# A fused attention and ternary feed-forward layer: loop skewed by one or two steps, token rows loaded before weights, output projection moved into the second feed-forward matmul

## The chip, the cores and the metric

One Trainium2 chip, all 8 NeuronCores; each core computes one of the 8 sequences of the batch (2048 tokens of 1024 features) and needs nothing from the others. The metric is the device time in microseconds of the slowest core. Shown is the median of three runs.

## The reference

```python
xn  = layernorm(x)                                  # x: (8, 2048, 1024)
q, k = xn @ Wq.T, xn @ Wk.T                         # 16 heads of 16 features
v   = xn @ Wv.T                                     # 16 heads of 64
f(z) = [1, z / 2, outer(z, z) / (4 * sqrt(2))]      # 273 features of a head
A   = tril(f(q) @ f(k).T)                           # (2048, 2048) for each head
y   = rms_norm(A @ v) * g_weight                    # over the 64 of each head
attn = y @ Wo.T
tern(W) = clip(round(W / s), -1, 1), s = max(mean(abs(W)), 1e-8)
ffn = gelu(xn @ tern(W1).T + b1) @ tern(W2).T + b2  # 1024 -> 4096 -> 1024
out = x + attn + ffn
```

## The kernel before, in words

The order of the work on each engine is written out by hand, one function an engine (`sync_stream`, `gp_stream`, `vec_stream`, `sca_stream`, `ten_stream`); semaphores connect them. DMAs are issued from SP (tokens, transposes, q blocks, stores) and from POOL (weights, which are cast from float32 to bfloat16 on the way when they go to `wqk`, `wv` and `wo`). Every queue is worked off in order: a wait at its head holds all that is behind it.

**Start.** SP loads token tiles of 128 rows into `xr` (three buffers); VectorE takes mean and variance (L447, L448, L450), ScalarE the root (L676), VectorE the reciprocal and the normalised rows `xn_tm` (L458), and SP transposes them by DMA into `xnT` (L264). The first projections (L772) need four tiles. POOL has issued all attention weights and the first two 1 MB staging loads by then (L348 to L373).

**Attention loop.** 32 iterations `i`: 16 chunks of 128 tokens for each half of the heads (8 heads). The sum over the past is held as a state in PSUM (`pST`), so a chunk needs its own 128 x 128 scores and the state before it. Iteration `i` on TensorE: scores of chunk i (L828); v (L784) and spread k (L793) of chunk i+1; y from the state (`y_before`, L841 to L853), spread q of i+1 (L804), y within the chunk (`y_within`, L862), spread q, update of the state (L872, L877), the small spread q (L815); in one iteration of four the q and k of the next block of four chunks (L772). ScalarE squares the scores (L722: a second-order polynomial by one square with bias), empties v, kx and the spread q (L681, L685, L691, L697), squares y (L735) and copies the state (L739). VectorE masks the squared scores (L586), makes the k features (`features_k`), raw q (L499), the sum of squares (L600), the scaled y (L511) and the second part of the state (L605). SP copies q into a block-diagonal `qblk` (eight copies a block, L275), which the scores read. All projections share two banks of `pW` in turn ("units": a table fixes their order; a unit waits until the one two before it is emptied).

In the loop ScalarE also sums the absolute values of `W1` (L709, `A1_SLOTS`, for the ternary threshold), and from iteration 18 on TensorE does the output projection of one finished chunk an iteration (`proj_out`, L891: 16 matmuls), VectorE adds x to it (`empty_wo`, L526) and SP writes the sum to DRAM (`res_scr`). Each y is transposed by DMA into `yT` (L282). The last two chunks' projections stand between the first steps of the next stage.

**Up** (`up`, L954): 32 steps `j` of 2 x 16 matmuls of `w1t`, the ternary weights that VectorE makes in two passes (L544, L547); ScalarE applies gelu (L751) into `hT` and sums absolute values of `W2`. Four PSUM pairs rotate.

**Down** (`down`, L977): for each half of the 1024 outputs, 16 groups `n` of 32 matmuls. The first eight groups run together, one step of `j` after another, each in a PSUM bank of its own; the other eight one after another. VectorE adds `b2` to what SP has read back from `res_scr` (L661), adds the PSUM bank (L667), and SP stores (L330). All 16 ternary `w2t` tiles but the last have their own place.

## Time and profile before

| | before |
|---|---|
| median of the runs | 809.74 us (805.32 to 813.83, 3 runs) |
| the profiled execution | 806.29 us, its slowest core's span 804.8 us |
| spans of the 8 cores | 799.1 to 804.8 us |
| mean granted clock of TensorE | 0.976 to 0.983 of full speed |
| TensorE, VectorE, ScalarE, GpSimd busy | 689.8 (86%), 376.4 (47%), 285.1 (35%), 40.6 us (5%) |
| DMA | 124.78 MB, mean 155 GB/s |

The span runs from the first to the last instruction of the slowest core. A busy share is the time in which at least one instruction of the engine is under way; matmuls are pipelined, so that several are under way together. The profile's line numbers (L828) are those of the kernel before.

### The profile page before, as it was taken

What the parts mean: (1) busy time and instruction counts of PE and PEld (TensorE: products, weight loads), DVE (VectorE), ACT (ScalarE), POOL (GpSimd) and SP (SyncE); (2) the same over time, 40 slices, a digit from 0 to 9 for tenths busy, and PEclk for the clock granted to TensorE, in tenths of its full rate; (3) what the DMA queues carried; (4) which work ended last, traced back from release to release, by engine and by line L of the source; (5) the groups of instructions that cost most, each with busy time, mean ns of one, the idle gap of its engine ahead of it and who ended that gap; (6) DMA issues with size and microseconds to landing.
All of it is one profiled execution on the core that took longest, in us unless ns stands there. A gap on an engine that the chain in (4) does not pass through costs nothing.

```text
span 804.8 us, 11638 instructions; the slowest of 8 cores (799.1 to 804.8 us)
## 1 busy us (share of the span) xinstructions
PE 689.8 (86%) x3996; PEld 330.3 (41%) x3996; DVE 376.4 (47%) x652; ACT 285.1 (35%) x432; POOL 40.6 (5%) x77
## 2 busy tenths in 40 slices
PE   0037776775899999879999999999999999999998
PEld 0013443442444444434444444444444444444443
DVE  4238886765666666752131314453366433300342
ACT  0006565673866765423556554333300000000000
POOL 2000000000000000000111111000010000000000
PEclk9999998998999999999999999999999999999999
DMA  8956674447679895663566664534154565100562
GB/s 150 235 128 134 129 137 104 145 88 155 179 227 240 218 246 150 170 205 110 198 233 210 224 216 189 177 136 158 53 187 135 175 157 157 53 1 1 140 165 88
DMA packets 62904, 124.78 MB, mean 155 GB/s; under 512 B 38528, under 2 KB 39552, under 8 KB 54272
## 3 DMA queue, kind: packets, MB, share of 16 engines
q0 software_dynamic: 10080, 72.62, 29.6%
q1 hardware_dynamic: 52768, 51.41, 25.8%
q8 instruction: 35, 0.57, 0.3%
q14 instruction: 21, 0.17, 0.1%
HBM read 103.30 MB, written 16.78 MB: 149 GB/s over the span
## 4 chain that ended last, share of the span: by engine, by line
PE 74%; DMA 9%; DVE 6%; issue 5%; ACT 3%; SPq 2%; DVEq 0%; ACTq 0%; POOL 0%; POOLq 0%
PE pW L891 7%; PE pST L954 7%; PE pSS L954 7%; PE pST L977 7%; PE pY L977 7%; PE pW L977 7%; PE pSS L977 7%; PE pY L954 6%; PE pW L954 6%; PE pW L784 4%; DMA xr<-x 4%; PE pW L772 2%; DMA wo_sb<-wo 2%; ACT qf L691 2%; SPq L275 2%
## 5 line engine op out<-in xcount | busy, mean ns | idle before, releaser
L772 PE MATMUL pW<-xnT,wqk_sb 128*128 128x512 bf16 x128 | 30.9, 398 | 57.6 <-DMA xnT<-xn_tm 51.6
L544 DVE TENSOR_SCALAR w1t<-stg,consts 128x2048 bf16<-128x2048 f32 x16 | 20.5, 1283 | 104.2 <-DMA stg<-w1r 84.8
L784 PE MATMUL pW<-wv_sb,xnT 128*128 128x512 bf16 x256 | 66.1, 405 | 0.4
L977 PE MATMUL pST<-w2t,hT 128*128 128x512 bf16 x256 | 66.0, 379 | 0.1
L977 PE MATMUL pW<-w2t,hT 128*128 128x512 bf16 x256 | 66.0, 379 | 0.0
L977 PE MATMUL pSS<-w2t,hT 128*128 128x512 bf16 x256 | 66.0, 379 | 0.0
L977 PE MATMUL pY<-w2t,hT 128*128 128x512 bf16 x256 | 66.0, 379 | 0.0
L709 ACT ACTIVATE stg<-stg 128x2048 f32<-128x2048 f32 x32 | 60.8, 1899 | 13.0 <-DMA stg<-w2r 13.0
L891 PE MATMUL pW<-wo_sb,yT 128*128 128x512 bf16 x256 | 60.7, 392 | 5.0 <-ACT qf L691 3.9
L954 PE MATMUL pST<-xnT,w1t 128*128 128x512 bf16 x272 | 61.5, 379 | 0.0
L954 PE MATMUL pSS<-xnT,w1t 128*128 128x512 bf16 x272 | 61.5, 379 | 0.0
L722 ACT ACTIVATE Am<-pSS,consts 128x1024 bf16<-128x1024 f32 x32 | 35.4, 1106 | 60.4 <-PE pSS L828 60.3
L954 PE MATMUL pY<-xnT,w1t 128*128 128x512 bf16 x240 | 54.2, 379 | 0.4 <-DVE consts L531 0.4
L954 PE MATMUL pW<-xnT,w1t 128*128 128x512 bf16 x240 | 54.2, 379 | 0.0
L661 DVE TENSOR_TENSOR res<-res,b2bc 128x512 f32<-128x512 f32 x32 | 22.1, 690 | 45.7 <-DMA res<-res_scr 45.5
L772 PEld LDWEIGHTS pW<-xnT,wqk_sb 128*128 128x128 bf16 x128 | 12.5, 101 | 73.4 <-issue 61.3
L784 PEld LDWEIGHTS pW<-wv_sb,xnT 128*128 128x128 bf16 x256 | 26.0, 104 | 38.1 <-issue 14.2
L544 DVE TENSOR_SCALAR w2t<-stg,consts 128x2048 bf16<-128x2048 f32 x16 | 20.5, 1283 | 44.2 <-PE pST L954 26.6
L691 ACT ACTIVATE qf<-pW 128x512 bf16<-128x512 f32 x64 | 35.0, 592 | 17.4 <-PE pW L804 17.1
L526 DVE TENSOR_TENSOR rst<-pW,xre 128x512 f32<-128x512 f32 x32 | 22.1, 691 | 38.5 <-PE pW L891 38.5
L891 PEld LDWEIGHTS pW<-wo_sb,yT 128*128 128x128 bf16 x256 | 24.9, 100 | 36.3 <-issue 10.3
L954 PEld LDWEIGHTS pSS<-xnT,w1t 128*128 128x128 bf16 x272 | 26.6, 98 | 32.1
(121 smaller groups left out, 921.5 us busy)
## 6 DMA issues: line engine op xcount, KB each, us to landing
stg<-w1r POOLq DMA_DIRECT2D x32, 1024.0 KB, 6.7
stg<-w2r POOLq DMA_DIRECT2D x32, 1024.0 KB, 6.2
xr<-x SPq DMA_DIRECT2D x16, 512.0 KB, 5.3
xre<-x SPq DMA_DIRECT2D x16, 512.0 KB, 6.1
res_scr<-rst SPq DMA_DIRECT2D x16, 512.0 KB, 4.3
res<-res_scr SPq DMA_DIRECT2D x32, 256.0 KB, 4.2
out<-osb SPq DMA_DIRECT2D x32, 256.0 KB, 2.7
wv_sb<-wv POOLq DMA_DIRECT2D x2, 1024.0 KB, 22.1
```

Of the source, the lines that this page charges most:

```text
L275: e.dma_start(out=qblk[16 * h:16 * h + 16, B % 2, h, :], in_=qT[16 * h:16 * h + 16, B % 2, :]).then_inc(dQB, 16)
L526: e.tensor_tensor(rst[:, c % 2, sl], work_bank(UID[key]), xre[:, c % 2, sl], ALU.add).then_inc(dW, 1)
L544: e.tensor_single_scalar(dst, src, cc(col + 1), ALU.is_lt).then_inc(sTA, 1)
L661: e.tensor_tensor(res[:, n % 2, :], res[:, n % 2, :], b2bc[:, dh * 512:dh * 512 + 512], ALU.add).then_inc(dRB, 1)
L691: e.activation(qf0[:, i % 2, 4 * half:4 * half + 4, :].rearrange("p h f -> p (h f)"), work_bank(UID[key]), AF.Square).then_inc(aW, 1)
L709: e.activation(buf, buf, AF.Abs, accum_out=cc(col)).then_inc(done, 1)
L722: e.activation(Am[:, b, :, :].rearrange("p h f -> p (h f)"), pSS[:], AF.Square, bias=cc(C_BI), scale=SC).then_inc(aSQ, 1)
L772: mm = e.matmul(work_bank(u), wqk[:, hf, kd, o:o + 128], xnT[:, 4 * b:4 * b + 4, kd, :], start=(kd == 0), stop=(kd == KD - 1))
L784: mm = e.matmul(work_bank(u), xnT[:, c, kd, :], wv[:, hf, kd, :], start=(kd == 0), stop=(kd == KD - 1))
L891: mm = e.matmul(work_bank(u), yT[:, c, k, :], wo[:, k, 512 * dh:512 * dh + 512], start=(k == 0), stop=(k == KD - 1))
L954: mm = e.matmul(ps[:, 512 * half:512 * half + 512], w1t[:, j % 6, kd, :], xnT[:, 4 * tb:4 * tb + 4, kd, :], start=(kd == 0), stop=(kd == K ...
L977: return e.matmul(out_bank(n), hT[:, j, 128 * t:128 * t + 128], w2t[8 * dh + j // 4][:, j % 4, :], start=(j == 0), stop=(j == NJ - 1))
```

## The change

- **Loop.** `scores(i + 1)` is issued in iteration i behind `outputs(i)` (which is `y_before` and `y_within` in one), v and kx of chunk i+2, `update(i)` first. v has three buffers. q is spread once for a block of four chunks: eight units `qf` of one 512-column matmul and a `qg` (q_units), in place of `qfa`, `qfb`, `qf1` in each iteration; raw q is copied by two DMAs from SP. `kx` of a chunk after which no state is needed is left out.
- **Layer norm.** The normalisation moves from VectorE to ScalarE (`normalise`, function Identity with scale and bias); `xr` has four buffers.
- **Start.** Token loads are the first DMAs on SP. On POOL come the iotas, the first half of q/k and v weights, four memsets that VectorE did before, then q blocks: half of block 0, blocks 1 and 2, with the second halves of the weights between, and only then the staging loads, with the other q blocks among them (`BEFORE_LOAD`).
- **Absolute sums.** The 16 of `W1` are at iterations 9 to 24, alternately on ScalarE and on VectorE (`tensor_reduce`).
- **Projection.** No `proj_out`, `empty_wo`, `res_scr`. y is stored to DRAM (`y_scr`, bfloat16); in the down stage it is read back by transposing DMAs, four tiles deep, once for each half of the outputs; after the 32 matmuls of a group come 8 of `yT` x `wo` in the same PSUM group (`attn`). `wo` is loaded and scaled half by half. x is read from the input in place of `res_scr`.
- **w2t.** Nine tiles have a place of their own; tiles 9 to 15 are made when the first half of the outputs is complete.

```diff
+def q_units(i, place):
+    if i == 0:
+        return {"first": [("qf", 4), ("qf", 5)], "mid": [("qf", 6)],
+                "last": [("qf", 7), ("qg", 0)]}[place]
+    B = i // 4 + 1
+    if B > 7:
+        return []
+    table = {1: {"first": [], "mid": [("qg", B)],
+                 "last": [("qf", 8 * B), ("qf", 8 * B + 1)]},
+             2: {"first": [("qf", 8 * B + 2)], "mid": [("qf", 8 * B + 3)],
+                 "last": [("qf", 8 * B + 4)]},
+             3: {"first": [("qf", 8 * B + 5)], "mid": [("qf", 8 * B + 6)],
+                 "last": [("qf", 8 * B + 7)]}}
+    return table.get(i % 4, {}).get(place, [])
+BEFORE_LOAD = {("a1", 0): ("b1", 0), ("a1", 2): ("q", 3), ("a1", 6): ("q", 4),
+               ("a1", 10): ("q", 5), ("a1", 14): ("q", 6), ("t1", 2): ("q", 7),
+               ("t2", 9): ("wo", 0), ("t2", 11): ("wo", 1)}
...
 def sync_stream(e):
-        e.dma_start(out=cc(C_G), in_=g_d).then_inc(dC, 16)
-        e.dma_start(out=consts[:, C_B1:C_B1 + 32], in_=b1_d).then_inc(dC, 16)
...
+        def y_in(n):
+            t = n % 16
+            if n >= 4:
+                e.wait_ge(pO, n - 3)
+            dYT.inc(e.dma_start(
+                out=yT[:, n % 4, :, :],
+                in_=y_scr[t * 128:(t + 1) * 128, :].rearrange(
+                    "p (b i) -> p b i", b=KD, i=128),
+                transpose=True), n)
...
         for n in range(32):
             final_out(n)
+            if n + 4 < 32:
+                y_in(n + 4)
             if n + 2 < 32:
-                res_in(n + 2)
+                x_again(n + 2)
...
 def gp_stream(e):
+        e.dma_start(out=wqk[:, 0, :, :], in_=wqk_d[0]).then_inc(dQK[0], 16)
         e.dma_start(out=wv[:, 0, :, :], in_=wv_d[0]).then_inc(dV[0], 16)
+        e.memset(qblk[:].rearrange("p a h t -> p (a h t)").bitcast(F32),
+                 0.0).then_inc(sMS, 1)
...
+        q_block(e, 0, range(4, 8), dQB)
+        q_block(e, 1, range(8), dQB)
         e.dma_start(out=wqk[:, 1, :, :], in_=wqk_d[1]).then_inc(dQK[1], 16)
+        q_block(e, 2, range(8), dQB)
         e.dma_start(out=wv[:, 1, :, :], in_=wv_d[1]).then_inc(dV[1], 16)
...
+            elif what == "wo":
+                if which == 0:
+                    e.wait_ge(pH, 2 * NJ)
+                else:
+                    e.wait_ge(pO, 16)
+                e.dma_start(out=wo[:], in_=wo_d[which]).then_inc(dWO[which], 16)
...
 def vec_stream(e):
         for i in range(NI):
+            if i + 1 < NI and has_state(i + 1):
+                features_k(i + 1)
+            if has_state(i):
+                state_out(i)
+            if new_block(i) is not None:
+                empty_qk("q", new_block(i))
+                empty_qk("k", new_block(i))
             for t in ln_tiles(i):
+                ln_stats(t)
+            if i >= 1:
+                rms_and_scale(i - 1)
+            for t in ln_tiles(i):
+                ln_scale(t)
+            sum_squares(i)
+            if i + 1 < NI:
+                mask(i + 1)
...
+            if n == 16:
+                for u in range(9, 16):
+                    ternary2(u)
+                scale_wo(1)
...
 def sca_stream(e):
         for i in range(NI):
+            if has_state(i):
+                e.wait_ge(pU, updates(i))
+                e.mul(st0[:, (i + 1) % 2, :], pST[:, 0:512], 1.0 / 32).then_inc(aS0, 1)
+            empty_q(q_units(i, "first"))
             e.wait_ge(pYD, i + 1)
             e.activation(ysq[:, b, :], pY[:, 512 * b:512 * b + 512],
                          AF.Square).then_inc(aYS, 1)
...
+            if i + 2 < NI:
+                empty_v(i + 2)
             if i + 1 < NI:
+                square(i + 1)
+            empty_q(q_units(i, "mid"))
+            if kx_chunk(i) is not None:
+                empty_kx(i + 2)
+            empty_q(q_units(i, "last"))
+            for t in ln_tiles(i):
+                normalise(t)
+            rms_sqrt(i)
...
 def ten_stream(e):
         for i in range(NI):
+            if has_state(i):
                 update(i)
+            if new_block(i) is not None:
+                proj_qk("q", new_block(i))
+                proj_qk("k", new_block(i))
+            spread_q(q_units(i, "first"))
+            outputs(i)
+            if i + 2 < NI:
+                proj_v(i + 2)
+            if i + 1 < NI:
+                scores(i + 1)
+            spread_q(q_units(i, "mid"))
+            if kx_chunk(i) is not None:
+                spread_k(i + 2)
+            spread_q(q_units(i, "last"))
...
+        def attn(n):
+            dh = n // 16
+            dYT.wait_done(e, n)
+            e.wait_ge(sWOG, KD * (dh + 1))
+            for k in range(KD):
+                mm = e.matmul(out_bank(n), yT[:, n % 4, k, :], wo[:, k, :],
+                              start=False, stop=(k == KD - 1))
+            mm.then_inc(pO, 1)
...
+            for n in range(n0, n0 + 8):
+                attn(n)
             for n in range(n0 + 8, n0 + 16):
                 down_free(n)
                 for j in range(NJ):
-                    mm = down(n, j)
-                mm.then_inc(pO, 1)
+                    down(n, j)
+                attn(n)
```

## Rows read from the trace of the kernel before

**Rows 1.** Windows by stage: length, busy us of each engine, granted clock, DMA share, GB/s.
```profile
0.00:26.00 26.00, 0.00 (x0) 0.00 (x0) 13.23 (x39) 1.87 (x3) 4.43 (x14) 1.00 0.91 161
26.00:51.60 25.60, 0.00 (x0) 0.01 (x1) 4.74 (x10) 0.59 (x2) 0.00 (x0) 1.00 0.95 229
51.60:128.70 77.10, 55.36 (x457) 28.41 (x457) 60.77 (x148) 43.10 (x88) 0.53 (x1) 0.97 0.62 130
128.70:220.40 91.70, 68.14 (x578) 36.59 (x579) 57.40 (x143) 63.30 (x114) 4.22 (x8) 0.90 0.52 128
220.40:351.40 131.00, 116.72 (x880) 61.53 (x879) 83.66 (x177) 73.52 (x128) 5.28 (x10) 0.97 0.78 206
351.40:580.20 228.80, 228.39 (x1060) 103.72 (x1059) 76.92 (x51) 101.66 (x96) 21.22 (x36) 1.00 0.51 177
580.20:805.00 224.80, 221.18 (x1025) 100.00 (x1022) 79.63 (x84) 1.11 (x1) 4.92 (x8) 1.00 0.39 113
```

**Rows 2.** Timeline, 0 to 60 us: start, duration in us, instruction, idle time before.
```profile
41.27 0.69 DVE L447 BATCH_NORM_STATS2 consts<-xr 128x6 f32<-128x512 f32 x1 [12.58 <-DMA xr<-x]
...
46.00 1.23 SPq L264 DMA_TRANSPOSE xnT<-xn_tm  x1
...
51.62 5.65 PE L772 MATMUL pW<-xnT,wqk_sb 128*128 128x512 bf16 x16 [51.62 <-DMA xnT<-xn_tm]
```

**Rows 3.** Timeline of TensorE in the attention loop.
```profile
62.53 0.97 PE L828 MATMUL pSS<-qblk,kT 128*128 128x512 bf16 x2 [1.11 <-DMA qblk<-qT]
...
128.74 1.01 PE L828 MATMUL pSS<-qblk,kT 128*128 128x512 bf16 x2 [5.15 <-DMA qblk<-qT]
...
220.40 3.62 PE L891 MATMUL pW<-wo_sb,yT 128*128 128x512 bf16 x16
```

**Rows 4.** Groups by form, ScalarE: count, busy us, mean ns, idle before.
```profile
L709 ACT ACTIVATE stg<-stg 128x2048 f32<-128x2048 f32 x32 | 60.8, 1899 | 13.0 <-DMA stg<-w2r 13.0
L722 ACT ACTIVATE Am<-pSS,consts 128x1024 bf16<-128x1024 f32 x32 | 35.4, 1106 | 60.4 <-PE pSS L828 60.3
L691 ACT ACTIVATE qf<-pW 128x512 bf16<-128x512 f32 x64 | 35.0, 592 | 17.4 <-PE pW L804 17.1 <-issue 0.2
...
L681 ACT CAST v<-pW 128x512 bf16<-128x512 f32 x32 | 18.5, 579 | 29.1 <-PE pW L784 29.0
...
L703 ACT ACTIVATE consts<-consts 128x8 f32<-128x8 f32 x32 | 9.3, 291 | 3.5 <-DVE consts L600 3.5
...
L676 ACT ACT_TABLE_LOAD x1 | 1.3, 1283 | 15.2 <-DVE consts L450 15.2
```

**Rows 5.** Groups by form, VectorE.
```profile
L547 DVE SCALAR_TENSOR_TENSOR w2t<-stg,consts,w2t 128x2048 bf16<-128x2048 f32 x16 | 37.6, 2352 | 2.0 <-DVE w2t L544 0.5
...
L544 DVE TENSOR_SCALAR w2t<-stg,consts 128x2048 bf16<-128x2048 f32 x16 | 20.5, 1283 | 44.2 <-PE pST L954 26.6 <-DMA stg<-w2r 17.6
...
L458 DVE TENSOR_SCALAR xn_tm<-xr,consts 128x1024 bf16<-128x1024 f32 x16 | 13.0, 812 | 1.7
```

**Rows 6.** Chain of waits, down stage: start, us, what; 64 matmuls in one piece.
```profile
773.82 13.81 PE pSS L977 x64
```

**Rows 7.** Timeline of VectorE after the first eight groups of down.
```profile
641.53 0.69 DVE L661 TENSOR_TENSOR res<-res,b2bc 128x512 f32<-128x512 f32 x1 [5.10 <-DMA res<-res_scr]
```

**Rows 8.** DMA issues: KB each, median us to landing.
```profile
wv_sb<-wv POOLq DMA_DIRECT2D x2, 1024.0 KB, 22.1
wo_sb<-wo POOLq DMA_DIRECT2D x1, 2048.0 KB, 19.2
wqk_sb<-wqk POOLq DMA_DIRECT2D x2, 512.0 KB, 15.0
...
xnT<-xn_tm SPq DMA_TRANSPOSE x16, 3.7
```

**Rows 9.** Groups by form, POOL's DMA issues.
```profile
L373 POOL DMA_DIRECT2D stg<-w2r x32 | 18.3, 571 | 198.3 <-DVE w2t L547 91.0 <-DVE w1t L547 74.2 <-ACT stg L709 33.1
```

**Rows 10.** Tile xn_tm, the DMA that reads it (the transpose into xnT).
```profile
DMA to landing us min/median/max: 3.1/3.7/16.7
```

More of the change, by code:

```diff
@@ L247, in ln_tiles, with q_block, x_in @@
         if i == 0:
[L248 to L250 removed]
+            return (6, 7)
+        if i <= 8:
+            return (i + 7,)
         return ()
+    def q_block(e, B, heads, done):
+        e.wait_ge(dW, D_DONE[UID[("q", B)]])
+        for h in heads:
+            e.dma_start(out=qblk[16 * h:16 * h + 16, B % 2, h, :],
+                        in_=qT[16 * h:16 * h + 16, B % 2, :]).then_inc(done, 16)
     def sync_stream(e):
[L255 to L258 removed]
+        def x_in(t):
+            dX.inc(e.dma_start(out=xr[:, t % 4, :],
+                               in_=x_d[t * 128:(t + 1) * 128, :]), t)
         def xn_out(t):
@@ L652, in vec_stream @@
         ternary1(15)
-        for u in range(3, 15):
+        for u in range(3, 9):
             ternary2(u)
+        e.wait_ge(dC, 32)
+        scale_wo(0)
         e.wait_ge(dB2, 16)
@@ L822, in scores @@
+        def scores(n):
+            B, c4 = n // 4, n % 4
             if c4 == 0:
-                e.wait_ge(dQB, 128 * (B + 1))
+                e.wait_ge(dQS, 64)
+                e.wait_ge(dQB, 64 + 128 * B)
                 e.wait_ge(dW, D_DONE[UID[("k", B)]])
-            if i >= 1:
-                e.wait_ge(aSQ, i)
-            for n in range(2):
-                mm = e.matmul(pSS[:, 512 * n:512 * n + 512],
+            if n >= 1:
+                e.wait_ge(aSQ, n)
+            for m in range(2):
+                mm = e.matmul(pSS[:, 512 * m:512 * m + 512],
@@ L873, in update @@
                          kf0[:, b, h, :, :].rearrange("p o i -> p (o i)"),
-                         v[:, b, E * h:E * h + E], start=(first and h == 0),
+                         v[:, i % 3, E * h:E * h + E], start=(first and h == 0),
                          stop=True, skip_group_check=True)
@@ L994, in ten_stream @@
                 for j in range(NJ):
[L995 to L996 removed]
+                    down(n, j)
+                attn(n)
     with ctx:
```

818 lines of the change are left out of this document (376 added, 442 removed).

## The prediction, made before the result was known

> **What bounds the kernel now.** I first cut the span into stages [rows 1]. TensorE starts at 51.6 us; the attention loop runs to 351.4, the first feed-forward matmul (up) to 580.2, the second (down) to the end. Both feed-forward stages are solid TensorE at full clock, 228.39 of 228.8 us busy and 221.18 of 224.8: they can only change by the number of matmuls. The rest is 351 us, and there TensorE is idle for the first 51.6 and then, in the three stretches of the loop, for 21.7, 23.6 and 14.3 us. "Busy" flatters it: a pipelined matmul shows as 0.4 us but streams 512 columns in 13.81/64 = 0.216 us [rows 6], so the loop has more slack than that, hidden in bubbles of small matmuls.
>
> Then the timeline. In the start [rows 2] VectorE gets the fourth token tile only at 41.27, after a wait of 12.58 us for its load; DMA is over 90% busy all that time [rows 1], carrying weights that nobody needs yet. The loop [rows 3]: scores of iteration 0 at 62.53, of iteration 8 at 128.74 (8.3 us an iteration, the last with a wait of 5.15 us for the q blocks), and the first output projection, of iteration 18, at 220.40: 157.9 us for 19 iterations. From 220.4 to 351.4 there are 14 pairs of output projections of 16 matmuls (16 x 0.216 = 3.45 us each, 48.3 in all), so the rest of these iterations takes 131.0 - 48.3 = 82.7 us, or 6.4 for each of 13.
>
> **Start.** Before TensorE's start DMA moves 26 x 161 + 25.6 x 229 GB/s = 10 MB [rows 1]. Of these, the second q/k and v weights, the bias row and two 1 MB staging loads now wait in POOL's queue behind copies of q blocks, which wait for q itself. Left are four tiles of 128 x 1024 in float32, 2.1 MB, and 1.5 MB of weights as landed [rows 8]: at 161 to 195 GB/s (the mean of the two) 19 to 23 us. So the fourth tile lands near 22; statistics 2 x 0.69 [rows 2], small operations about 1, the scaling 1.1, the transpose 3.7 (median) to 5.6 (issued at 46.00, used at 51.62) [rows 2, 8]: TensorE starts at 30, bounds 26 (tokens landing before the weights) and 38 (a transpose that lands in 12 us, within the 16.7 of [rows 10]). **-21.6 us.** The memsets that move to POOL are covered as long as they end before the q blocks are filled, some 30 us later.
>
> **Loop.** The skew puts scores one iteration ahead and k features and v two, so that TensorE no longer waits for square, mask and features in one chain; the pace is then set by the fullest engine.
> - ScalarE, each iteration [rows 4]: square of scores 1.11, v 0.58, kx, ysq and state of the same 512 columns and so 0.6 each, q features 2 x 0.59, the root of the rms 0.3; sum 4.97. New: the small q features, two instructions a block of four iterations, of at most 0.59 us: 0.3 an iteration, sum 5.25. In the first nine iterations a root 0.3 and the normalisation that DVE loses: no row has it on ScalarE; between 0.59 (512 wide) and 1.90 (2048 wide), nearest the 1024 wide square, 1.1. Sum 6.65. In iterations 9 to 24 every second one carries an absolute sum, 1.90 and its read-out 0.2: 1.05 on average, sum 6.3. Back-to-back instructions overlap a little, some 0.06 each, so 6.1, 5.8 and 4.8.
> - VectorE had 60.77 busy us in the first stretch [rows 1], some 7 an iteration; it loses 0.81 (scaling) and 0.43 (raw q, now two small copies on SP): about 6. Later it takes eight absolute sums; no row has such a reduction of 2048; between 1.28 (a 2048 wide operation) and 2.35 [rows 5], 2.2 because its reductions run one element a cycle like the latter: 1.1 an iteration, on 4.1 (6 less the statistics): 5.2.
> - TensorE: v 1.73, the rest some 11 streams of 512 columns, 2.4, and q and k 3.45 in one iteration of four: 5.0 on average but 8 in that one, which nothing can overtake because the two work banks are shared.
> The iterations with q and k are TensorE's (8.0), the others ScalarE's or VectorE's (6.0 to 7.0). I take 6.8, 6.5 and 5.8 for the three phases (9, 16 and 7 iterations, the last with two ternary stalls): 61 + 104 + 41 = 206, and 14 ahead of it (before 10.9; one more v and kx, clock at half): 220 us, bounds 190 (TensorE's own 5.0 with half an us of bubbles each) and 245. Before it is 299.8 - 48.3 = 251.5 without projections. **-31.5 us.** Most comes from the first half; in the second the projections were also cover, under which ScalarE did its absolute sums, so that removing 48.3 us there doesn't bring 48.3 by itself; that is in the 206.
>
> **Projection.** Moved, not removed: 256 matmuls, 55.2 us, out of loop (48.3) and up (6.9), into down. **0.** VectorE's 32 additions of 0.69 us and the residual's trip to DRAM go, all hidden.
>
> **Down, its waits.** After the first eight groups, eight projections of 1.73 us follow at once, but only four transposed tiles fit. Load 4 waits for projection 0; loads 6 and 7 stand in SP's queue behind the store of outputs 2 and 3, which wait for an addition that waits for x. That round trip is in the trace: after two quick evictions the third waits 5.10 us for its load [rows 7]. Counted from the start of projection 0: it ends at 1.7, is evicted at 2.6, SP issues store, transpose and x load until 4.5; x lands some 5 later, the addition and eviction of output 2 take 1.4, so load 6 is issued at about 11.5 us and load 7 at 13.5. With a landing of L the last projection ends at 15.2 + L, against 13.8 unhindered, so the loss is L + 1.4. L is 3.7 at the median for the same shape out of SBUF, 3.1 at least and 16.7 at most [rows 8, 10]; from DRAM it has no row. With 4.2, near the median, 5.6 us, and some at half clock: 6 each, twice. **+12 us** (9 to 36). The second half's loads of `w2` now come after the first half is done; VectorE makes one in 1.28 + 2.35 = 3.6 us, TensorE uses one in 6.9. The tightest is the third new one, whose load starts at 4.5 us and must be ternary at 20.7, behind 1 MB of landed `wo`; cover 2 us. If `wo` took its 19.2 us of before [rows 8], it costs 9.
>
> **Sum.** 804.8 - 21.6 - 31.5 + 12 = 763.7 of span; its execution took 1.5 more than the span, and the median of the runs is 0.4% above it: **767 us**.
>
> **ScalarE's tables.** The row shows one load of 1.28 us for roots, squares, copies and absolute values together [rows 4]. The normalisation adds a function, Identity. The Trainium skill, ScalarE: Activation LUTs, section "Table sets: the hidden batching unit", says that such cheap functions are in every set, so no load is added. If it were otherwise, 16 tiles with two loads each are 41 us, most of them seen: 805.
>
> **Rivals.**
> 1. TensorE's pace: the loop reaches 5.5 an iteration, 190 in all: 767 - 30 = 737. For it: slack averages out over four iterations. Against: two work banks, both emptied by ScalarE in strict order. 0.13.
> 2. ScalarE or VectorE in the way: the bubbles between engines stay, 7.2 an iteration: 245, so 792. For it: ScalarE is at 6.65 of work in the first phase, 1 us more than now. 0.14.
> 3. The start isn't earlier: x loads stay slow because a queue gives them the same share beside the weights; TensorE at 45: 782. Against: the weights are a third as many. 0.07.
> 4. Slower: q blocks through POOL. Sixty of the 64 small copies leave SP for POOL's queue. In the trace POOL issues a DMA in 0.57 us [rows 9], with VectorE busy 64% of the last loop stretch [rows 1], so eight take 4.6 us; some 13 us lie between q and the scores that need it. It decides from 13/8 = 1.6 us an issue. Were each issue held by one ternary operation of 2.35 us [rows 5], it took 2.9, eight 23.4, and TensorE waited 10 us in each of seven blocks: 767 + 73 = 840; over 817 from 2.5 us an issue on. 0.03. The Trainium skill, SBUF — State Buffer, section "SBUF: two separate sides", says that GpSimd can't write descriptors while a two-port VectorE operation runs, and gives 3100 ns in place of 620, by which the sum would be about 850. By that rule some of the issues beside these operations should be long; the trace doesn't show it, their mean is 571 ns [rows 9].
> 5. Nothing gained in the loop (8.3 for 19 iterations, 7.4 for 13, 14 ahead): 268, 815. 0.04.
>
> Forecast's own case 0.59, 750 to 784.
>
> **Numbers.** The range 738 to 795 takes in rivals 2 and 3 and the edge of 1, and leaves out about 0.17. A change under 1% (8 us) can't be told from none. Faster 0.91 (all but 4 and 5, and mixtures of 2 and 3), same 0.05 (most of 5, and those mixtures), slower 0.04 (4, and the tail of 5).
>
> **What would show it.** First matmul near 30 us; first up matmul near 250; loop iterations of about 6.5 us with ScalarE over 85% busy; two gaps of some 3 us between projections near 560 and 700 on DMA into `yT`; up unchanged at 221; no second table load in the loop. Wrong if TensorE waits for `qblk` (rival 4), if the loop ends before 230 (1) or after 270 (2, 5), or if the transposes take over 10 us.

## The result

| | before | after |
|---|---|---|
| median of the runs | 811.79 us (4 runs of the same session) | 845.44 us (840.98 to 848.08, 4 runs) |
| ratio | | 1.044, interval 1.035 to 1.053 |
| span of the profiled execution, slowest core | 804.8 us | 839.4 us (the eight: 830.0 to 839.4) |
| first matmul, median of the cores | 50.6 us | 32.1 us |
| loop, TensorE's start to the up stage, median of the cores | 298.8 us | 279.8 us |

The kernel became 4% slower; 767 us were forecast. Here and below the ratios leave out runs in which the cores of one die took longer at a lower granted clock, so that a median can lie above what its ratio says. The same windows as [rows 1] for the kernel after, the loop cut at its waits (length, then busy us of TensorE, its weight loads, VectorE, ScalarE and POOL, granted clock, DMA share, GB/s):

```profile
0.00:32.00 32.00, 0.00 (x0) 0.01 (x1) 16.98 (x49) 7.51 (x10) 6.61 (x13) 1.00 0.96 205
32.00:47.60 15.60, 11.05 (x36) 3.98 (x37) 5.89 (x17) 5.71 (x10) 1.93 (x4) 1.00 0.26 65
47.60:107.00 59.40, 35.64 (x235) 16.37 (x236) 31.70 (x87) 36.65 (x63) 4.37 (x9) 0.79 0.49 115
107.00:147.40 40.40, 26.55 (x185) 12.37 (x184) 23.14 (x62) 24.01 (x42) 7.04 (x14) 0.84 0.69 140
147.40:210.00 62.60, 49.50 (x349) 23.78 (x349) 35.34 (x74) 42.16 (x71) 11.43 (x23) 0.90 0.39 127
210.00:270.00 60.00, 45.30 (x352) 22.68 (x353) 40.28 (x87) 42.50 (x72) 11.43 (x23) 0.94 0.50 165
270.00:317.20 47.20, 32.77 (x287) 17.24 (x285) 34.45 (x72) 28.09 (x51) 5.98 (x12) 0.96 0.30 98
317.20:540.70 223.50, 223.09 (x1028) 100.94 (x1026) 74.36 (x47) 102.68 (x98) 21.16 (x36) 0.99 0.49 175
540.70:839.40 298.70, 279.19 (x1280) 124.70 (x1278) 83.11 (x100) 1.11 (x1) 5.84 (x10) 0.99 0.56 120
```

Against [rows 1], core 4 in both: the start gave 19.6 us, the loop 14.6 (299.8 to 285.2), up 5.3, and down lost 73.9; in sum 34.4 more, the difference of the spans (34.6) but for rounding. Against the forecast of 763.7 us for this span, 75.7 us are too many: 2.0 in the start (32.0 for 30), 65.2 in the loop (285.2 for 220), 1.6 in up (223.5 for 228.8 - 6.9 = 221.9) and 6.9 in down (298.7 for what the forecast left it, 763.7 - 30 - 220 - 221.9 = 291.8). In the loop no engine is full: ScalarE reaches 71% (over 85% was forecast), VectorE 73%, TensorE 79%.

TensorE's timeline, the projections of q for a block of four (idle time before, and who ended it):

```profile
32.02 6.25 PE L849 MATMUL pW<-xnT,wqk_sb 128*128 128x512 bf16 x16 [32.02 <-DMA xnT<-xn_tm]
69.51 6.28 PE L849 MATMUL pW<-xnT,wqk_sb 128*128 128x512 bf16 x16 [8.69 <-DMA xnT<-xn_tm]
106.91 6.35 PE L849 MATMUL pW<-xnT,wqk_sb 128*128 128x512 bf16 x16 [5.61 <-DMA xnT<-xn_tm]
147.44 6.56 PE L849 MATMUL pW<-xnT,wqk_sb 128*128 128x512 bf16 x16 [6.23 <-DMA xnT<-xn_tm]
```

The first answers to 51.62 in [rows 2]. The other three had no counterpart: q of the next block is now projected where `i % 4` is 1 and reads row tiles up to 4B+3, but tile i+7 is normalised at the end of iteration i, so the last tile is one iteration old and its transpose still on its way. Behind each wait of 6 to 9 us the 16 matmuls take 6.3 to 6.6 us; the four later blocks, without such a wait, take 3.61 us each, at full clock.

Blocks whose rows are there are slow as well. Starts of the scores (L900), with the longest wait between two of them:

```profile
217.72 0.59 PE L900 MATMUL pSS<-qblk,kT 128*128 128x512 bf16 x2
...
221.22 0.38 PE L882 MATMUL pW<-qT,L 128*128 128x512 bf16 x1 [1.70 <-ACT qf L768]
...
226.91 0.59 PE L900 MATMUL pSS<-qblk,kT 128*128 128x512 bf16 x2
```

Around them the scores start at 208.00, 217.72, 226.91, 233.44 and 240.12 us: 9.7 us with q and k, 9.2 for the iteration after it, then 6.5 and 6.7. The plain iterations are as forecast (6.0 to 7.0); the one with q and k was forecast at 8.0, and the slow one behind it was not in the forecast.

Then who TensorE waits for in the loop (line, releaser; us in total, times, longest): the kernel after from 32.1 to 317 us, then the kernel before from 51.7 to 351.4. The first row of each counts from the span's start.

```profile
PE pW L849 <- DMA xnT<-xn_tm: 52.5, 4, 32.0
PE pW L882 <- ACT qf L762: 19.9, 16, 2.6
PE pW L882 <- ACT qf L768: 12.0, 7, 1.8
PE pW L870 <- ACT v L747: 9.1, 21, 2.5
PE pW L861 <- DVE qT L525: 5.3, 4, 1.4
```
```profile
PE pY L862 <- DVE Am L586: 14.2, 3, 8.3
PE pSS L828 <- DMA qblk<-qT: 11.4, 4, 5.2
PE pW L815 <- ACT qf L691: 9.5, 10, 1.4
PE pW L804 <- ACT v L681: 7.5, 7, 1.9
PE pW L772 <- ACT qf L691: 6.0, 7, 1.2
PE pW L891 <- ACT qf L691: 3.9, 9, 0.5
```

The waits on q blocks are gone, as meant, and those on masks fell from 14.2 to 1.6 us. In their place stand the rows (20.5 us in the loop) and, at L882 (`spread_q`), the two banks of pW that ScalarE has to empty: 32 us in 23 waits. All waits for an emptied bank of pW together went from 28.7 to 50.2 us. The loop in one window (TensorE's idle time is 285.00 - 200.61 = 84.4 us; before it was 59.6):

```profile
32.00:317.00 285.00, 200.61 (x1440) 96.26 (x1441) 170.62 (x398) 179.11 (x306) 42.19 (x85) 0.89 0.45 126
```

### The profile page after: what moved, and what is told of

It reads as the page before. It is cut to its first block, busy times and chain, and to the rows that moved or that the text cites. A ratio compares the mean times of both kernels' runs of the same rounds, so it can differ in the third digit from the quotient of the medians.

```text
span 839.4 us, 11098 instructions; the slowest of 8 cores (830.0 to 839.4 us)
## 1 busy us (share of the span) xinstructions
PE 703.1 (84%) x3746; PEld 322.1 (38%) x3746; DVE 345.2 (41%) x594; ACT 290.4 (35%) x415; POOL 75.8 (9%) x144
## 4 chain that ended last, share of the span: by engine, by line
PE 71%; DMA 10%; issue 6%; DVE 5%; ACT 5%; SPq 1%; ACTq 0%; DVEq 0%; POOL 0%; POOLq 0%
PE pSS L1018 7%; PE pST L1018 7%; PE pY L1018 7%; PE pW L1018 7%; PE pSS L1032 6%; PE pST L1032 6%; PE pW L1032 6%; PE pY L1032 6%; PE pW L861 5%; DMA xnT<-xn_tm 5%; PE pW L849 4%; DMA stg<-w2r 2%; PE pW L882 2%; PE pY L1040 1%; PE pSS L1040 1%
## 5 line engine op out<-in xcount | busy, mean ns | idle before, releaser
L849 PE MATMUL pW<-xnT,wqk_sb 128*128 128x512 bf16 x128 | 39.9, 481 | 54.3 <-DMA xnT<-xn_tm 52.5
L861 PE MATMUL pW<-wv_sb,xnT 128*128 128x512 bf16 x256 | 60.5, 379 | 6.2 <-DVE qT L525 5.3
L1018 PE MATMUL pW<-xnT,w1t 128*128 128x512 bf16 x256 | 57.9, 379 | 0.0
L882 PE MATMUL pW<-qT,L 128*128 128x512 bf16 x64 | 27.8, 441 | 34.5 <-ACT qf L762 19.9
L779 ACT ACTIVATE stg<-stg 128x2048 f32<-128x2048 f32 x24 | 45.7, 1904 | 9.1 <-DMA stg<-w2r 9.1
L606 DVE TENSOR_SCALAR w2t<-stg,consts 128x2048 bf16<-128x2048 f32 x16 | 20.5, 1283 | 61.3 <-DMA stg<-w2r 34.7
L849 PEld LDWEIGHTS pW<-xnT,wqk_sb 128*128 128x128 bf16 x128 | 14.5, 118 | 77.9 <-issue 70.9
L288 POOL DMA_DIRECT2D qblk<-qT x60 | 28.7, 487 | 137.9 <-DVE qT L525 137.9
L609 DVE SCALAR_TENSOR_TENSOR w1t<-stg,consts,w1t 128x2048 bf16<-128x2048 f32 x16 | 37.6, 2352 | 1.7
L609 DVE SCALAR_TENSOR_TENSOR w2t<-stg,consts,w2t 128x2048 bf16<-128x2048 f32 x16 | 37.6, 2352 | 1.7
L1032 PEld LDWEIGHTS pSS<-w2t,hT 128*128 128x128 bf16 x256 | 25.0, 98 | 34.4 <-issue 4.7
L559 DVE TENSOR_TENSOR Am<-Am,tril 128x1024 bf16<-128x1024 bf16 x32 | 22.1, 692 | 38.0 <-ACT Am L773 38.0
## 6 DMA issues: line engine op xcount, KB each, us to landing
wv_sb<-wv POOLq DMA_DIRECT2D x2, 1024.0 KB, 15.1
```

The costliest lines, as they stand in the source:

```text
L288: e.dma_start(out=qblk[16 * h:16 * h + 16, B % 2, h, :], in_=qT[16 * h:16 * h + 16, B % 2, :]).then_inc(done, 16)
L559: e.tensor_tensor(Am[:, n % 2, :, :], Am[:, n % 2, :, :], tril[:].unsqueeze(1).broadcast_to([128, 8, 128]), ALU.mult).then_inc(dMK, 1)
L606: e.tensor_single_scalar(dst, src, cc(col + 1), ALU.is_lt).then_inc(sTA, 1)
L609: e.scalar_tensor_tensor(dst, src, cc(col), dst, ALU.is_gt, ALU.subtract).then_inc(done, 1)
L779: e.activation(buf, buf, AF.Abs, accum_out=cc(col)).then_inc(done, 1)
L849: mm = e.matmul(work_bank(u), wqk[:, hf, kd, o:o + 128], xnT[:, 4 * b:4 * b + 4, kd, :], start=(kd == 0), stop=(kd == KD - 1))
```

## Experiments

Short names are those of the expectations: a_ is the kernel after with an edit, b_ the kernel before. Each was timed in three rounds beside the kernel before. The ratio of the kernel after has an interval of 0.009 to either side (7 us), so small steps are read from the loop, TensorE's start to the up stage, as the median of eight cores: 298.8 us before, 279.8 after (the expectations say 299 and 279.6).

**Rows of block 0 for every block of the first half** (q and k of blocks 1 to 3 are then those of block 0). a_old_rows:

```diff
-            hf, b = B // 4, B % 4
+            hf, b = B // 4, B % 4 if B > 3 else 0
```


> The changed kernel, with the q and k projections of blocks 1 to 3 reading the normalised rows of block 0 in place of their own (that part of the values is not the reference's; the number and the shapes of all instructions are the same). So TensorE never waits for a row tile that has only just been normalised. Theory A (the next block's q and k are asked for in the iteration in which their last tile is normalised; in the trace three waits for the transpose of 8.7, 5.6 and 6.2 us, and matmuls at half clock behind them): the three iterations shrink from 24.4, 15.7 and 18.8 us to about 9.1, as the later ones with q and k: 31 us less, about 814, the first up matmul at 286. Rival R (ScalarE, with the normalisation, or VectorE has too much to do in the first nine iterations, and the wait is only where it shows): the work comes out elsewhere, under 12 us less, over 833.

821.24 us, ratio 1.015 (1.013 to 1.017); loop 258.5 us, 21.3 less. The wait on rows, with the clock behind it (0.94 in this loop, 0.89 with the waits), costs that much; expected were 31. TensorE is idle for 68.0 of 261.2 us on its core 7 even so, 50.3 of them for an emptied bank of pW: those waits stayed as they were.

**Shorter squares of the spread q units** (7/8 of their features are left out from block 2 on). a_short_qf:

```diff
-                    e.activation(qf0[:, n // 8 % 2, n % 8, :], bank,
+                    w = 512 if n < 16 else 64
+                    e.activation(qf0[:, n // 8 % 2, n % 8, 0:w], bank[:, 0:w],
```


> The changed kernel, with ScalarE squaring only 64 of the 512 columns of each spread q unit of blocks 2 to 7 (the rest of these features isn't written, so part of the values is not the reference's); matmuls and order as they are. Theory B (two work banks, each to be emptied by ScalarE in its strict order, make TensorE wait in the two iterations that take a new block: in the trace 12.0 us of waits on these squares in three blocks, and half clock behind them): 4 to 6 us a block, 24 to 36 in six blocks: 803 to 815. Rival (the chain scores, square, mask, y sets the iteration, or TensorE itself): under 8 us less, over 837.

848.4 us, ratio 1.035 (1.027 to 1.042); loop 270.2, 9.6 less. ScalarE's busy time in the loop fell by 21.6 us (179.1 to 157.5), the loop by under half of it. The squares hold TensorE up in part; theory B's 24 to 36 us didn't come.

**Only the start changed.** b_rows_first, with the token loads as SP's first DMAs, and on POOL:

```diff
+        e.wait_ge(sXN, 4)
         e.dma_start(out=wqk[:, 1, :, :], in_=wqk_d[1]).then_inc(dQK[1], 16)
```


> The kernel before, with the start alone changed: the token loads are SP's first DMAs, and on POOL everything behind the first halves of the q/k and v weights waits until four tiles are normalised. Everything else as before. If rows first, weights later is worth by itself what the start of the changed kernel shows (first matmul at 32.0 in place of 51.6 us): ratio 0.976 to 0.980, about 792. Rival (the loads that are put off then collide with the loop's, whose DMAs took over 60% in the first iterations): half of it comes back, 800 to 805.

814.7 us, ratio 1.005 (1.002 to 1.008): neither theory. TensorE started at 53.9 us. Timeline of POOL, SP and TensorE, and windows of the same core:

```profile
28.82 0.53 POOL L358 DMA_DIRECT2D wqk_sb<-wqk  x1 [25.67 <-DVE xn_tm L459]
...
29.43 3.13 SPq L264 DMA_TRANSPOSE xnT<-xn_tm  x1
...
53.90 4.43 PE L773 MATMUL pW<-xnT,wqk_sb 128*128 128x512 bf16 x10 [53.90 <-DMA xnT<-xn_tm]
```
```profile
26.00:32.00 6.00, 0.00 (x0) 0.00 (x0) 1.96 (x5) 0.29 (x1) 2.65 (x5) 1.00 0.34 73
32.00:40.00 8.00, 0.00 (x0) 0.00 (x0) 0.00 (x0) 0.00 (x0) 0.00 (x0) 1.00 1.04 176
```

The weights went out 0.6 us ahead of the last transpose, the DMA engines were full (share 1.04), and the transpose landed 24.3 us after its issue.

**Weights released by the landing of that transpose.** b_rows_landed:

```diff
         e.wait_ge(sXN, 4)
+        dXT.wait_done(e, 2)
+        dXT.wait_done(e, 3)
```


> The kernel before with the rows loaded first, as in the last such kernel, but the second halves of the weights and all behind them wait until the transposes of row tiles 2 and 3 have landed, not only until the tile is normalised. In the last one those loads went out at 28.8 us, the DMA engines were full (share 1.02 from 32 to 54 us), and the last transpose, issued at 29.4 us, landed 24.3 us later. Theory A: the transposes land in 3 to 5 us, TensorE starts at 32 to 36 us instead of 50.6, and the loop behind it takes its 299 us: 792 to 799 us. Rival R (the loop waits for what now comes later, the second halves and the first tiles of the feed-forward weight, and gives the start back): TensorE starts early too, but the time is over 805 us.

799.1 us, ratio 0.987 (0.981 to 0.992), the upper edge of theory A. TensorE starts at 34.8, 15.8 us earlier; the loop grew by 7.6, to 306.4: its first scores now wait 6 to 9 us for q blocks, which are on their way at the same time as those weights (1.11 us in [rows 3]). Half of what the start gains the loop takes back.

**An eighth of the projection in the loop of the kernel before** (the rest left out). b_short_proj: one of eight matmuls in each unit of `proj_out`.

> The kernel before, with one matmul in place of eight in every output projection unit (so seven eighths of the projection are left out): 224 matmuls of 0.216 us, 48.3 us of TensorE, of them 42.3 in the loop. If the second half of the loop is TensorE's alone: 48 less, ratio 0.940, 762. If the projections were cover for ScalarE's absolute sums and for the chain between the engines, as the forecast took it in part: the loop gives back 10 to 25 us, 772 to 787.

788.96 us, ratio 0.974 (0.971 to 0.977), 21.4 us less. In the loop 7/8 of 222 matmuls at 0.216 us, 42.0 us, returned 20.0 (278.8 against 298.8). Its core 4, then the kernel before, the loop in one window:

```profile
51.00:324.70 273.70, 195.83 (x1688) 107.24 (x1719) 198.56 (x466) 178.92 (x329) 10.07 (x19) 0.94 0.66 175
```
```profile
51.60:351.40 299.80, 240.22 (x1914) 126.53 (x1915) 201.84 (x468) 179.92 (x330) 10.03 (x19) 0.95 0.66 163
```

On this core TensorE's busy time fell by 44.4 us, its idle time rose from 59.6 to 77.9. The waits at L891, the projection's own turn at the two banks, went from 5.0 to 16.6 us, most of it here:

```profile
PE pW L891 <- ACT qf L697: 13.8, 9, 1.6
```

**The second feed-forward matmul alone.** a_down:

```diff
+            if n % 16 == 0:
+                for m in range(n + 4, n + 8):
+                    y_in(m)
...
-            if n + 4 < 32:
+            if n % 16 >= 4 and n + 4 < 32:
...
-                ("t2", 9): ("wo", 0), ("t2", 11): ("wo", 1)}
+                ("t2", 9): ("wo", 0), ("t2", 14): ("wo", 1)}
```


> The kernel after; only the second feed-forward matmul changes: the transposing loads of attention rows 4 to 7 and 20 to 23 are issued by SP ahead of the first stores of the output instead of behind them, and the second half of the output projection's weight is loaded behind two more tiles of the second feed-forward weight. Theory A (each burst of eight accumulation groups stops for the attention rows queued behind the stores, 7.4 us in 4 waits, and the tile of the weight that comes 4.05 us late does so because 1 MB goes ahead of it; together with the clock behind them some 9 to 11 us): 834 to 838 us. Rival R (the stores and the evictions that free the banks set these waits, and the rows would only wait elsewhere): 842 us or more.

838.27 us, ratio 1.033 (1.029 to 1.038), 7 us less, though the intervals of the two ratios overlap; the stage itself took 294.5 us for 298.9, 4.4 less. The 4.1 us on `w2t` went, and within the two bursts 0.5 us of waiting on rows is left of 12.0. But the row tile of the ninth group is now the one that stands behind the stores, and TensorE waits for it in each half (4.50 and 4.71 us), with half clock behind:

```profile
621.50 3.57 PE L1043 MATMUL pSS<-wo_sb,yT 128*128 128x512 bf16 x8 [4.50 <-DMA yT<-y_scr]
```

So the rows do wait for the stores, as theory A has it, and most of that wait was only moved.

**q, k and spread units one iteration later.** a_block_later: `new_block` where `i % 4` is 2, `q_units` shifted to 2, 3 and 0, POOL's q blocks 3 to 6 one staging load later.

> The kernel after, but the q and k projection of the next block of four and the spread units behind it come one iteration later (where i mod 4 is 2), so that the last of its four row tiles is normalised an iteration before it is read. Theory A (the wait for that row tile costs the loop some 21 us, as the kernel with old rows showed: median loop of a core 258.6 us against 279.6): that wait falls from about 20 us to under 3, the loop takes 255 to 265 us, the time is 820 to 827 us. Rival R (the block's chain q/k, copy, spread, square is what TensorE waits for, wherever it stands; one iteration later it has an iteration less before its features are read): new waits on the spread q units or on the q blocks take the place of the wait on rows, the time is over 835 us.

834.75 us, ratio 1.028 (1.025 to 1.032): between the two, next to rival R. Loop 269.8, 10 less. The wait on rows shrank from 20.5 to 5.7 us, and a new one of 15.2 us at the outputs (L925) is for the last square of the block: half of the 21 us is only moved.

**v projected twice.** a_double_v:

```diff
-            for kd in range(KD):
+            for kd in list(range(KD)) * 2:
```


> The kernel after with every projection of v computed twice in the same PSUM group (the second start overwrites the first): 32 x 8 more matmuls of 512 columns in the loop, 55.3 us of TensorE at 0.216 us, as much as the output projection had in the loop of the kernel before. Theory A (the loop's pace is set by a chain of engines that hand each other work, with TensorE idle for a third; work added to TensorE is partly covered, as in the kernel before, where taking 48.3 us out returned 21.4 us, 0.44 of it): 24 to 32 us more than the kernel after, 868 to 878 us. Rival R (in the skewed loop TensorE's own order is the bound and all added work is paid): 50 to 56 us more, 894 to 902 us.

903.44 us, ratio 1.114 (1.109 to 1.120); loop 339.6, 59.8 more for 55.3 us of matmuls. That is rival R's price: lengthened in place, a unit is paid in full, and the waits behind it stay (L882 31.3 us).

**The same work as units of its own**, `extra` being eight matmuls of v's shape into a work bank. a_fill:

```diff
+            extra(i)
             spread_q(q_units(i, "mid"))
...
+            unit_filled(e, ("fx", i))
+            e.tensor_copy(fxo[:, i % 2, :],
+                          work_bank(UID[("fx", i)])).then_inc(dW, 1)
```


> The kernel after with one more unit an iteration in its loop, between the scores and the spread q unit: eight matmuls of 512 columns into a bank of pW (55.3 us of TensorE in all), emptied by VectorE with a copy (about 0.7 us), as the output projection was in the kernel before; what they compute is not used. Theory A (the skewed loop covers about half of work that stands between two hand-overs, as the old loop did): 22 to 34 us more than the kernel after, 867 to 880 us, TensorE's waits at the spread q units (L882, 34.5 us) falling by half. Rival R (all of it is paid, as the doubled v projection was, 58 us): 895 us or more.

877.5 us, ratio 1.080 (1.073 to 1.087); loop 308.9, 29.1 more: theory A, 53% paid. The waits at `spread_q` (L895 there) for ScalarE to empty a bank fell from 34.3 to 9.9 us, while 20.2 us of waits on VectorE's copy (L666) are new:

```profile
PE pW L883 <- DVE fxo L666: 17.0, 21, 1.0
...
PE pW L895 <- ACT qf L773: 3.1, 7, 0.4
PE pW L895 <- ACT qf L767: 2.6, 1, 2.6
```

Its loop on core 4:

```profile
32.60:345.00 312.40, 246.88 (x1665) 118.93 (x1697) 189.89 (x430) 183.26 (x308) 42.20 (x85) 0.93 0.43 119
```

TensorE's idle time fell from 84.4 to 65.5 us, and its busy time rose by 46.3 us and not by 55.3, at a granted clock of 0.93 for 0.89: some 19 us of the cover are waits that shrank and 9 are the clock. So the skewed loop covers about half of such work just as the old one did; it isn't TensorE's order as such that makes work cost its full length. From a_double_v this kernel differs in the place of the work and in who empties the bank (VectorE, not ScalarE); the runs don't separate the two.

**An eighth of the projection in down** (the rest left out). a_short_attn: `for k in (0,)` in `attn`.

> The kernel after; of the eight matmuls by which the output projection joins each accumulation group of the second feed-forward matmul only the first is issued (the output leaves 7/8 of the projection out): 32 x 7 matmuls, 48.4 us of TensorE at 0.216 us. Theory A (in that stage TensorE is all but full, nothing covers them): 47 to 50 us less than the kernel after, about 796 us. With the 21.4 us that the same 48.4 us cost in the loop of the kernel before, the move itself then loses 27 us. Rival R (the groups wait for attention rows and evictions anyway, so part of the projection was covered): under 40 us less, above 804 us.

819.87 us, ratio 1.011 (1.006 to 1.017), 26 us less, not 48: rival R. The stage took 268.8 us for 298.9, 30.1 less. TensorE's waits from 540 us, the kernel after and then this one:

```profile
PE pY L1040 <- DMA yT<-y_scr: 7.4, 4, 2.4
PE pW L1040 <- DMA yT<-y_scr: 4.6, 4, 1.7
PE pSS L1032 <- DVE w2t L609: 4.1, 1, 4.1
```
```profile
PE pW L1040 <- DMA yT<-y_scr: 15.8, 4, 6.0
PE pY L1040 <- DMA yT<-y_scr: 14.6, 4, 4.4
PE pSS L1032 <- DVE w2t L609: 5.2, 2, 4.2
```

The matmuls of a burst cover the landing of the next row tiles; without them 18.4 us more of waiting on rows shows, and the granted clock falls to 0.91 (600 to 700 us) and 0.83 (700 to 760). So this isn't the price of the projection in down: as it shortens the matmuls it lengthens the waits for their operands. a_hybrid, below, has neither.

**Rows one iteration earlier, on top of a_down.** a_both: tiles 8 and 9 in iteration 1, then i+8.

> The kernel with the changed second feed-forward matmul (attention rows ahead of the first stores, weight half later; ratio 1.033), and in its loop the row tiles are normalised one iteration earlier from iteration 1 on (8 and 9 in iteration 1, then i+8), so that the q and k projections of blocks 2 and 3 find their last row tile; block 1's tile 7 stays where it was. Theory A (waits on rows 5.61 and 6.23 us at 106.9 and 147.4 us go, with the half clock behind them; the 8.7 us at 69.5 us stays): 8 to 14 us less than with the second matmul's change alone, 824 to 830 us. Rival R (what the extra tile in iteration 1 adds to ScalarE and VectorE, or the chain behind the q projection, takes it back): 835 us or more.

829.96 us, ratio 1.022 (1.015 to 1.029); loop 272.6, 7.4 less than a_down's 280.0. Theory A, at the low end of its gain; 8 us less in all.

**Skew and early start without the move, a stand-in.** a_hybrid: a_fill with the rows of a_both and no projection matmul in down (left out).

> A stand-in for skew and early start without the move: the extra units of the last kernel in the loop, row tiles one iteration earlier from iteration 1 on, and the second feed-forward matmul without any matmul of the output projection (left out; the loads of its operands stay). Theory A (the move lost, the skew and the start gained): TensorE at 32, loop 290 to 298 us, up 223.5, down as in the kernel before 225 to 232: 775 to 787 us, under both kernels. Rival R (the skewed loop pays for all work that is added, loop 322 us or more): 805 us or more.

803.24 us, ratio 0.991 (0.988 to 0.995): neither. The loop took 300.4 us, 27.8 over a_both's, so rival R's reason fell; but down took 240.7 us (median of the cores, 247 on the slowest) instead of the 224.7 of the kernel before. The chain that ends last there goes through x's landing (from 615.71 to 672.44 seven pieces of 4.16 to 10.24 us), each followed by VectorE's addition and SP's next issue. Against the kernel after it is 43 us less, some 7 of them by the rows. Two prices come out of it. Down without any projection matmul is 53.3 us shorter than a_both's (294.0) and 58.2 shorter than the kernel after's (298.9), though its slowest core waits 16.6 us for evictions: there the 55.2 us of the projection cost about their full length. And with 55.3 us of extra units the skewed loop takes 300.4 us, where the old one took 298.8 with 48.3 us of projection.

**Four kernels after b_rows_landed.** b_best: four q blocks of block 0 through POOL, and `wo` scaled in iteration 16 instead of 14.

> The kernel before with rows loaded first and weights released when the fourth transpose has landed (799.1 us), and two waits of its loop taken away: four of the eight q blocks of the first block go through POOL's queue (the first scores waited 8.57 us for them, issued one behind the other in 5.0 us), and the output projection's weight is scaled two iterations later (VectorE stood 7.9 us for its landing, the masks behind it held TensorE 9.27 us). Theory A: 2 to 3 us and 7 to 10 us less: 787 to 791 us. Rival R (the loop's chain takes such waits back, as it covered 56% of the projection's work): above 795 us.

807.73 us, ratio 0.995 (0.992 to 0.998): rival R, and worse than without them by 8. The wait on masks went (15.1 to 6.4 us), but POOL's half of the q blocks stood in one queue with the weights and held the first scores for 15.9 us. b_wo_later has the later scaling alone:

> The kernel with rows first and weights behind the fourth transpose (799.1 us, ratio 0.987), with only the scaling of the output projection's weight on VectorE moved from iteration 14 to 16. In the last kernel, where the q blocks' half went through POOL too, TensorE's wait on the masks fell from 15.1 to 6.4 us, but the first scores waited 15.9 us for those blocks behind the weights. Theory A: the 8 to 9 us on the masks go and nothing else changes: 789 to 793 us. Rival R (the loop takes it back): 797 us or more.

802.81 us, ratio 0.991 (0.988 to 0.994): rival R. The 2 MB load of `wo` was issued at 154.5 us and landed 19.7 us later. Timeline of SP and TensorE behind it:

```profile
184.16 10.87 SPq L282 DMA_TRANSPOSE yT<-ytm  x2
```
```profile
189.80 1.01 PE L831 MATMUL pSS<-qblk,kT 128*128 128x512 bf16 x2 [19.11 <-DMA qblk<-qT]
```

The wait on the scaling had only stood ahead of one on a transpose (14.7 us on VectorE, until 183.35) and on q blocks. b_q_landed holds the weights until the q blocks have landed, b_wo_parts also loads `wo` in three parts:

> The kernel with the scaling of the projection's weight in iteration 16 (802.8 us), but POOL holds the second halves of the weights and all behind them until the eight q blocks of the first block have landed, not only until the fourth transpose has. Theory A: the first scores wait under 2 us for the q blocks instead of 5.5, and the next loads of rows are not slowed either: 4 to 8 us less, 795 to 799 us. Rival R (the loop gives it back in the 19.1 us wait of iteration 16): 801 us or more.

> The kernel b_q_landed, with the output projection's weight (2 MB) loaded in three parts before the fifth, sixth and seventh tile of the first feed-forward weight instead of at once before the seventh. The trace of the kernel with the later scaling has SP's transposes held 10.9 us and VectorE 14.7 us on one of them behind that load, and then 19.1 us of TensorE's wait on q blocks. Theory A (2 MB at once fill the queues in front of a transpose): that wait falls to under 8 us, the time by 8 to 14 us, 783 to 790 us. Rival R (the bytes hold the transposes however they are cut): 794 us or more.

805.41 us, ratio 0.991 (0.988 to 0.993), and 804.0 us, ratio 0.991 (0.988 to 0.994): rival R in both. The first scores waited 1.5 and 0.4 us, but both traces have a new wait of 11.0 us on VectorE, at 72.6 and at 75.0 us, and waits on q blocks of 15.3 us at 190.9 in b_q_landed, of 5.4 and 8.9 us in b_wo_parts. In b_wo_parts the longest wait on q blocks did shrink, from 19.1 to 8.9 us, close to what theory A asked, and the time didn't. No edit behind b_rows_landed gained anything; of the kernels that leave nothing out it is the fastest of the study, 1.3% under the kernel before.

## Why the prediction was wrong

- **Start: right.** 32.0 us for 30. What the prediction didn't look at is the transpose beside the weights: b_rows_first has it and starts at 53.9 us. The kernel after escapes it because its second weights stand behind q blocks in POOL's queue.
- **Loop: wrong, the step that failed.** It said 220 us, "the pace is then set by the fullest engine"; measured 279.8 (median of the cores). Three parts make the 59.8:
  - *The projection's 48.3 us*, taken off in full to get 251.5. At b_short_proj's rate (20.0 of 42.0; an estimate, for the whole of it) they return 23.0, which leaves a loop of 275.8: 24.3 us (1.0 less than 48.3 - 23.0, because the 251.5 start from core 4's 299.8 and not from the median, 298.8). The prediction wrote that removing 48.3 doesn't bring 48.3 and that this is "in the 206"; no term of the 206 is for it.
  - *The skew and all else that was changed in the loop*, forecast at 31.5 us: from 275.8 to the 258.5 of a_old_rows they brought 17.3, which is 14.2 us short.
  - *The rows*, not in the prediction: 21.3 us. Which iteration reads which row tile was never laid against which iteration makes it.

  The first two are one error. An engine's sum is a lower bound, and here no engine came near it: TensorE waited for an emptied bank of pW for 28.7 of its 59.6 idle us in the kernel before and for 50.2 of 84.4 in the kernel after. As the waits on masks and q blocks went, those at the banks grew, and they stand in the two iterations of four that take and spread a new block (9.7 and 9.2 us at 208 to 227 us, the others 6.5). The prediction had one such iteration, of 8.0, and the two banks only as an argument against rival 1.
- **Projection, moved for 0: wrong, the same error seen from the other end.** Down paid it about in full, as forecast (53.3 for 55.2, a_hybrid against a_both). What it left didn't give it back: the loop 23.0 of 48.3, up 5.1 of 6.9 (228.6 to 223.5). So by these prices the move alone costs some 25 us (53.3 - 23.0 - 5.1; an estimate). In either loop such work costs about half its length (b_short_proj, a_fill), in a stage where TensorE is busy for 221 of 225 us all of it.
- **Down's waits, +12: right, in mechanism and size.** 12.0 us in 8 waits on row tiles, 6.0 in each of two bursts (at 604 to 615 and 754 to 765 us), and a_down shows that the stores ahead of the loads set them. The stage is 6.9 us over: 4.1 are the wait on a late `w2t` tile, the fourth new one (the prediction had looked at the third, with a cover of 2 us; the fourth's load took 19 us beside `wo`, with the DMA engines full), the rest is longer busy time (279.2 for 221.2 + 55.2).
- **Up: right**, 223.5 for 221.9.
- **Sum.** The scaling at its end is a little off: 763.7 + 1.5, with 0.4% on top, is 768, not 767.
- **Rivals.** 2 (bubbles stay, 792) and 5 (nothing gained in the loop, 815) were nearest, with 0.14 and 0.04. Rival 2 still let the projection's 48.3 us leave the loop in full; rival 5 kept some 17 of them (268 for 251.5). Neither had the rows, and so neither came to 845. The prediction's own sign of being wrong for these two, a loop that ends after 270 us, did show: it ended at 317. Rival 4, the only slower one, didn't occur: POOL issued its 60 q blocks in 0.48 to 0.51 us each, with VectorE 53 to 73% busy, and TensorE never waited for one (the lock that the Trainium skill, SBUF — State Buffer, section "SBUF: two separate sides", describes for such issues doesn't show).
- **Smaller prices.** ScalarE's normalisation 1.24 us for 1.1, VectorE's absolute sum 2.28 for 2.2, transposes from DRAM 4.1 for 4.2. What the price of the normalisation leaves out is a wait: ScalarE stood 8.2 us for landing transposes before it (its buffer is read by them), with the loop's squares and copies behind it in the same queue. ScalarE's groups by form in the kernel after, and POOL's:

```profile
L740 ACT ACTIVATE xn_tm<-xr,consts 128x1024 bf16<-128x1024 f32 x16 | 19.7, 1239 | 12.0 <-DMA xnT<-xn_tm 8.2 <-DVE consts L518 3.8
L724 ACT ACT_TABLE_LOAD x1 | 1.3, 1283 | 1.5 <-DVE consts L453 1.5
L827 ACT ACT_TABLE_LOAD x1 | 1.3, 1283 | 3.4 <-PE pSS L1018 3.4
```
```profile
L288 POOL DMA_DIRECT2D qblk<-qT x60 | 28.7, 487 | 137.9 <-DVE qT L525 137.9
```

Two table loads, one at the start (L724) and one for gelu (L827), none beside the normalisation (L740). The Trainium skill, ScalarE: Activation LUTs, section "Table sets: the hidden batching unit", says that Identity is in every set; by that rule none was to be expected, and the trace agrees.

**Left open.** That the two banks are why the changes in the loop gave 17.3 and not 31.5 is read from the waits, with a_short_qf (21.6 us off the squares gave 9.6) and a_fill beside them; it isn't shown by a kernel with a third bank for pW, which wasn't tried. Nor was the skew run without the other changes of the loop. How far a better down stage would bring a_hybrid wasn't tried either.

## What to carry to other kernels

Work on the fullest engine isn't full price everywhere: before it is moved, leave it out once where it stands. Here 42 us out of the loop gave 20, and in its new place TensorE was already busy for 98% of the stage. A sum of busy times bounds a loop from below; where TensorE idles at hand-overs between engines, a part of the work that is taken away comes back as idle time (18.3 of 44.4 us of busy time here). And when a loop is skewed, write down for each operand the iteration that makes it and the one that reads it: one such line would have shown the rows.

## What the runs showed of the hardware

VectorE's small copies at the start, and POOL's memsets beside them, in the kernel after (start, duration), and the first of these copies in the kernel before, where POOL ran no memset beside it:

```profile
2.51 5.08 DVE L463 COPY L<-Ix 128x128 bf16<-128x128 bf16 x1
...
7.55 0.19 DVE L473 COPY KX<-Ix 128x192 bf16<-128x192 bf16 x1
```
```profile
9.78 0.19 DVE L417 COPY L<-Ix 128x128 bf16<-128x128 bf16 x1
```
```profile
2.84 3.54 POOL L395 MEMSET qblk<- 128x4096 f32 x1
6.29 0.98 POOL L397 MEMSET qf<- 128x1024 f32 x1
```

A copy that takes 0.19 us took 5.08 while POOL filled tiles, and the three VectorE instructions behind it took 4.3 to 5.0: all four ended at 7.6 us, when POOL's large memsets had. The start didn't wait for them, as the fourth row tile landed only at 22.1 us. The Trainium skill, SBUF — State Buffer, section "SBUF: two separate sides", calls the ports that VectorE and GpSimd share an exclusive lock, held for a whole instruction by whichever starts first. The trace agrees that one of the two blocks the other outright; that the copy's record starts 0.3 us ahead of the memset's it doesn't explain. In the other direction, POOL's issues beside VectorE, no run here shows a cost (0.49 us an issue).

In b_rows_first a transpose by DMA that was issued 0.6 us behind the first of 3.8 MB of weights, on another queue, landed in 24.3 us, against 4.0 at the median of that run: a queue of its own didn't protect it. In b_rows_landed, where the weights waited for that transpose, TensorE started at 34.8 us and not at 53.9.
